# Projections of an attention block: four product banks, one copy for both query tiles, waits for the transposes moved ahead of a product's last matmul

## The reference

```python
x = x + _L0_conv_ref(_gn(x), L0_conv_w, L0_conv_b)        # mixes points inside shifted 8x8 windows
x = x + _L1_conv_ref(_gn(x), ...)

def _L1_conv_ref(x, w_qkv, w_dw, w_pw, w_proj, bn_gamma, bn_beta, bn_mean, bn_var):
    qkv = jnp.einsum('bchw,oc->bohw', x, w_qkv)            # 256 -> 768 channels
    y = lax.conv_general_dilated(qkv, w_dw, ...)           # 5x5, each channel by itself
    y = lax.conv_general_dilated(y, w_pw, ...)             # 1x1 in groups of 8 channels
    mqkv = jnp.concatenate([qkv, y], axis=1)               # 64 heads of 8 channels, N = 4096
    q = relu(mqkv[:, :, :DIM]); k = relu(mqkv[:, :, DIM:2 * DIM]); v = mqkv[:, :, 2 * DIM:]
    v = jnp.pad(v, ((0, 0), (0, 0), (0, 1), (0, 0)), constant_values=1.0)
    vk = jnp.einsum('bhdn,bhen->bhde', v, k)               # sums over all points
    out = jnp.einsum('bhde,bhen->bhdn', vk, q)
    out = out[:, :, :-1] / (out[:, :, -1:] + ATT_EPS)
    ...                                                    # projection, batch norm
```

## Time and profile before

| | us |
|---|---|
| three runs | 2472.43, 2471.01, 2472.25 |
| median | 2472.25 |
| span of the profiled execution | 2473.8 |
| projections in it, first to last product's matmul | 266.9 to 999.3 |
| TensorE busy in the whole span | 2359.6 (95%) |
| VectorE, ScalarE, GpSimd busy in the whole span | 1994.9 (81%), 1495.6 (60%), 1099.8 (44%) |

### The profile page before, as it was taken

One profiled execution on the slowest core, in us unless ns is written; L12 is line 12 of the kernel. 1 busy time (PEld: TensorE's weight loads), 2 busy tenths in 40 slices (PEclk: granted clock), 3 DMA queues, 4 the chain that ended last, 5 costly groups with the idle time before them and its releaser, 6 DMA issues. The chain is left out here.

```text
span 2473.8 us, 66794 instructions
## 1 busy us (share of the span) xinstructions
PE 2359.6 (95%) x25485; PEld 1881.3 (76%) x25485; DVE 1994.9 (81%) x2653; ACT 1495.6 (60%) x1864; POOL 1099.8 (44%) x1476
## 2 busy tenths in 40 slices
PE   5999799999999999799999999999999889999998
PEld 5889688877777887577888888888888656666666
DVE  7887688878788877778888888888888588888775
ACT  5777566666566666566776776677767434433442
POOL 7722387887787878200000000000000068888887
PEclk9999899999999999899999999999999999999999
DMA  7874689988988989988888888888888777777774
GB/s 285 336 301 173 208 295 344 329 293 314 316 288 323 344 299 302 253 196 207 209 209 208 209 210 207 210 208 209 207 208 210 228 243 280 275 275 271 271 272 136
DMA packets 300973, 628.38 MB, mean 254 GB/s; under 512 B 50784, under 2 KB 252256, under 8 KB 291552
## 3 DMA queue, kind: packets, MB, share of 16 engines
q1 hardware_dynamic: 295072, 590.38, 77.5%
q10 hardware_dynamic: 4688, 31.63, 3.6%
q0 software_dynamic: 1008, 3.67, 0.4%
HBM read 327.81 MB, written 300.94 MB: 254 GB/s over the span
## 5 line engine op out<-in xcount | busy, mean ns | idle before, releaser
L1562 PE MATMUL c_ps<-dh,wh 128*128 128x512 f32 x1152 | 465.3, 404 | 15.8 <-DVE wl L1712 9.9
L1477 ACT ACTIVATE dh<-image 128x1632 fp32r<-128x1632 f32 x192 | 301.5, 1570 | 269.9 <-PE c_ps L1562 254.8
L1562 PE MATMUL c_ps<-dh,wl 128*128 128x512 f32 x1152 | 456.4, 396 | 0.0
L1562 PE MATMUL c_ps<-dl,wh 128*128 128x512 f32 x1152 | 454.6, 395 | 1.6 <-issue 1.6
L1921 POOL TENSOR_TENSOR ql<-image,qh 128x1024 fp32r<-128x1024 f32 x1 | 2.4, 2359 | 967.8 <-DVE ql L2152 967.8
L1670 DVE TENSOR_TENSOR dl<-image,dh 128x1632 fp32r<-128x1632 f32 x192 | 356.3, 1856 | 73.9 <-ACT dh L1477 73.9
L1132 PE MATMUL o_ps<-xh,wqh 128*128 128x512 f32 x768 | 319.2, 416 | 11.3 <-issue 8.4
L1909 POOL TENSOR_TENSOR ql<-image,qh 128x1024 fp32r<-128x1024 f32 x126 | 300.9, 2413 | 10.7 <-ACT qh L1940 10.7
L1132 PE MATMUL o_ps<-xl,wqh 128*128 128x512 f32 x768 | 303.5, 395 | 0.0
L1132 PE MATMUL o_ps<-xh,wql 128*128 128x512 f32 x768 | 301.9, 393 | 0.0
L1562 PEld LDWEIGHTS c_ps<-dh,wh 128*128 128x128 f32 x1152 | 218.5, 190 | 68.6 <-DVE wl L1712 10.0
(11 more groups left out here) (212 smaller groups left out, 5107.8 us busy)
## 6 DMA issues: line engine op xcount, KB each, us to landing
qkv_scratch<-stage SPq DMA_DIRECT2D x384, 408.0 KB, 4.7
image<-qkv_scratch SPq DMA_DIRECT2D x189, 816.0 KB, 6.3
yq_scratch<-qy SPq DMA_DIRECT2D x64, 512.0 KB, 6.7
image<-qr_scratch SPq DMA_DIRECT2D x128, 256.0 KB, 6.1
image<-yq_scratch SPq DMA_DIRECT2D x128, 256.0 KB, 5.3
ox<-x_scratch SPq DMA_DIRECT2D x8, 4096.0 KB, 15.3
qr_scratch<-qs SPq DMA_DIRECT2D x126, 256.0 KB, 3.6
out<-ox SPq DMA_DIRECT2D x7, 4096.0 KB, 12.7
```

The lines of the kernel that those rows point to most:

```text
L1477: act.activation(dh[kind][:, :], raw[kind], ACT.Copy).then_inc(hi_ready, 1)
L1562: last = pe.matmul(c_ps[:, m, :], w[hp][:, kind, part, o:o + P], cells[:, :, HALF * dy:HALF * dy + HALF * NB], start=(k == 0), stop=(k == 5))
```

## The change

- `o_ps` has four banks; product j of step n goes to bank (6n + j) % 4. The waits for a free bank change with it: product 0 waits for `kv_ready` of the step before, product 1 for `kv_ready_v`, products 2 and 3 for `q_ready`, product 4 for `kv_ready` and product 5 for `kv_ready_v` of the same step.
- `vk_ps` is now a part of one bank (`psum_ps` in the rows of after), with one start flag for both head groups.
- Both query tiles are copied by one instruction on ScalarE of 1024 elements, after product 5 and after `turned(1)`. VectorE's copy and the semaphore `q_ready_v` are gone.
- `pause` is gone on GpSimd. `edge` is now a tensor_tensor with a broadcast zero as its other operand, and carries the waits itself. `border` follows the first edge of the step.
- The four waits of `turn` stand ahead of the sixth matmul of the product before it (products 2 and 4), so that the eight transposes have no wait of their own.

```diff
-        o_ps = psum("o_ps", [P, 3, 512])
+        NO = 4
+        o_ps = psum("o_ps", [P, NO, 512])
...
-        vk_ps = psum("vk_ps", [P, 2, 512])
+        sum_bank = psum("psum_ps", [P, 512])
+        vk_ps = sum_bank[:, 0:2 * VS].rearrange("p (u n) -> p u n", u=2)
...
+        def bank(n, j):
+
+            return (QT * n + j) % NO
...
                         if n % 2:
-                            pool.tensor_scalar(staged(j0, n, 0, 0, 1), every_second(buf, t0, n, 0, 1), -1.0, None, ALU.mult)
+                            pool.tensor_tensor(staged(j0, n, 0, 0, 1), none, every_second(buf, t0, n, 0, 1), ALU.subtract)
                         else:
-                            pool.tensor_copy(staged(j0, n, 1, HALF - 1, HALF), every_second(buf, t0, n, NB - 1, 1))
+                            pool.tensor_tensor(staged(j0, n, 1, HALF - 1, HALF), every_second(buf, t0, n, NB - 1, 1), none, ALU.add)
...
                         keys_values_free(pool, b, n)
-                        pause(1 + u, n)
+                        if u == 0 and n % 4 < 2:
+                            queries_free(pool, b, n)
                         edge(kv, 2 * u, 2 * u, n)
+                        if u == 0 and n % 4 < 2:
+                            border(n)
...
                         pool.wait_ge(q_ready, g + 1)
-                        pool.wait_ge(q_ready_v, g + 1)
                         queries_free(pool, b, n)
                         at_least(pool, K["qr_stored"][n % 2], 32 * (4 * b + n // 2))
-                        pause(3, n)
...
-                        act.wait_ge(o_full, o0 + 5)
+                        turned(1)
+                        act.wait_ge(o_full, o0 + 6)
                         queries_read(act, g)
-                        act.activation(qw[:, n % 2, 0, :], o_ps[:, 1, :], ACT.Copy).then_inc(q_ready, 1)
-                        turned(1)
+                        act.activation(qw[:, n % 2, :, :], o_ps[:, bank(n, 4):bank(n, 4) + 2, :], ACT.Copy).then_inc(q_ready, 1)
...
-            def product(b, n, j):
+            def product(b, n, j, before_last=None):
...
                     for w, xx in ((wh, xh), (wl, xh), (wh, xl)):
-                        last = pe.matmul(o_ps[:, j % 3, :], w[:, ct, P * t:P * t + P], xx[:, n % 2, ct, :],
+                        if k == 5 and before_last:
+                            before_last()
+                        last = pe.matmul(o_ps[:, bank(n, j), :], w[:, ct, P * t:P * t + P], xx[:, n % 2, ct, :],
...
-            def turn(b, n, u):
-
-
+            def turn_ready(b, n, u):
                 at_least(pe, k_turned, 2 * (NCH * b + n) + u)
                 at_least(pe, v_turned, 2 * (NCH * b + n) + u)
                 pe.wait_ge(kv_ready, 2 * (NCH * b + n) + u + 1)
                 pe.wait_ge(kv_ready_v, 2 * (NCH * b + n) + u + 1)
+
+            def turn(n, u):
...
-                        product(b, n, 2)
-                        turn(b, n, 0)
+                        product(b, n, 2, lambda: turn_ready(b, n, 0))
+                        turn(n, 0)
...
-                        product(b, n, 4)
+                        product(b, n, 4, lambda: turn_ready(b, n, 1))
...
-                        turn(b, n, 1)
+                        turn(n, 1)
...
-                        dve.wait_ge(o_full, QT * g + 6)
-                        queries_read(dve, g)
-                        dve.tensor_copy(qw[:, n % 2, 1, :], o_ps[:, 2, :]).then_inc(q_ready_v, 1)
```

More of the change, by code:

```diff
@@ L767, in projections @@
         vT = sb("vT", [P, 2, 4, NSQ, VS])
-        tick = sb("ptick", [P, 4 * NCH])
+        zero = sb("zero", [P, 1])
         pw_rep = sb("pw_rep", [P, QT, NPH, D])
@@ L790, in projections @@
         kv_ready, q_ready = sem("kv_ready"), sem("q_ready")
-        kv_ready_v, q_ready_v = sem("kv_ready_v"), sem("q_ready_v")
+        kv_ready_v = sem("kv_ready_v")
         kv_diff, kv_odd = sem("kv_diff"), sem("kv_odd")
@@ L891, in _ @@
         def _(pool):
+            pool.memset(zero[:, :], 0.0).then_inc(zeroed, 1)
             pool.memset(vT[:, :, :, :, SQ:VS], 1.0).then_inc(zeroed, 1)
+            pool.wait_ge(zeroed, 2)
+            none = zero[:, :].unsqueeze(1).unsqueeze(2).broadcast_to([P, 4, NB, 1])
             def body(i, last_body):
@@ L896, in body @@
                     b = 2 * i + par
-                    def pause(k, n):
-                        k = NCH * k + n
-                        pool.tensor_tensor(tick[:, k:k + 1], K["ident"][:, 0:1], K["ident"][:, 1:2], ALU.add)
                     def border(n):
                         row = NB * (1 - n // 4)
-                        keys_values_free(pool, b, n)
-                        queries_free(pool, b, n)
-                        pause(0, n)
                         pool.memset(stage[:, n % 2, :, :, :, row, :].rearrange("p t a k x -> p (t a) k x"), 0.0)
@@ L942, in body @@
                     for n in range(NCH):
-                        if n % 4 < 2:
-                            border(n)
                         keys_values(n, 0)
@@ L1045, in key @@
                                 cells_free(act, g)
-                            act.activation(kv[:, n % 2, 2 * u, :], o_ps[:, (2 * u) % 3, :], ACT.Copy).then_inc(kv_ready, 1)
+                            act.activation(kv[:, n % 2, 2 * u, :], o_ps[:, bank(n, 2 * u), :], ACT.Copy).then_inc(kv_ready, 1)
                         def turned(u):
@@ L1073, in body @@
                             pointwise(2)
-                        act.wait_ge(o_full, o0 + 5)
+                        turned(1)
+                        act.wait_ge(o_full, o0 + 6)
                         queries_read(act, g)
-                        act.activation(qw[:, n % 2, 0, :], o_ps[:, 1, :], ACT.Copy).then_inc(q_ready, 1)
-                        turned(1)
+                        act.activation(qw[:, n % 2, :, :], o_ps[:, bank(n, 4):bank(n, 4) + 2, :], ACT.Copy).then_inc(q_ready, 1)
                         if last_body and par == 1 and n == NCH - 1:
                             act.wait_ge(q_ready, g + 1)
-                            act.wait_ge(q_ready_v, g + 1)
                             act.wait_ge(K["qr_stored"][n % 2], 32 * (4 * b + n // 2))
@@ L1107, in _ @@
                 last.then_inc(w_turned, 1)
-            pe.wait_ge(zeroed, 1)
-            def product(b, n, j):
+            pe.wait_ge(zeroed, 2)
+            def product(b, n, j, before_last=None):
                 t = TILES[j]
@@ L1116, in product @@
                 if j == 0:
+                    at_least(pe, kv_ready, 2 * (NCH * b + n))
+                if j == 1:
                     at_least(pe, kv_ready_v, 2 * (NCH * b + n))
+                if j == 2 or j == 3:
                     at_least(pe, q_ready, NCH * b + n)
-                if j == 1:
-                    at_least(pe, q_ready, NCH * b + n)
-                if j == 2:
-                    at_least(pe, q_ready_v, NCH * b + n)
-                if j == 3:
+                if j == 4:
                     pe.wait_ge(kv_ready, 2 * (NCH * b + n) + 1)
-                if j == 4:
+                if j == 5:
                     pe.wait_ge(kv_ready_v, 2 * (NCH * b + n) + 1)
-                if j == 5:
-                    pe.wait_ge(kv_ready, 2 * (NCH * b + n) + 2)
                 k = 0
@@ L1158, in sum_vk @@
                         last = pe.matmul(vk_ps[ch, u, 0:VS], kT[:, u, a, ch], vT[:, u, a, q, :],
-                                         start=(n == 0 and a == 0), stop=(n == NCH - 1 and a == 3))
+                                         start=(n == 0 and u == 0 and a == 0), stop=(n == NCH - 1 and u == 1 and a == 3))
                 if u == 1:
@@ L1276, in value @@
                             cells_free(dve, g)
-                        dve.tensor_copy(kv[:, n % 2, 2 * u + 1, :], o_ps[:, (2 * u + 1) % 3, :]).then_inc(kv_ready_v, 1)
+                        dve.tensor_copy(kv[:, n % 2, 2 * u + 1, :], o_ps[:, bank(n, 2 * u + 1), :]).then_inc(kv_ready_v, 1)
                     def keys_values(n, u):
@@ L1288, in queries @@
                         dve.wait_ge(q_ready, g + 1)
-                        dve.wait_ge(q_ready_v, g + 1)
                         queries_free(dve, b, n)
```

## The result

The changed kernel takes 2485.68 us (median of 4 runs, 2483.11 to 2488.47) against 2471.99 us before (4 runs, 2471.01 to 2472.43): a ratio of 1.0057, 95% interval 1.0044 to 1.007. It is slower by 14 us. The prediction had said 2480 within 2467 to 2492, and slower as the likeliest. So the forecast was +8 us and the runs give +14, at the upper edge of its main case (2475 to 2486).

A forecast was written before the change was run, and what follows sets the result against it. TensorE, busy 98 to 100% in both stretches, was taken to set the stage's end by its own order. The terms 9.2 - 1.0 - 1.5 - 0.5 - 1.4 + 3.2 = +8.0 us gave a median of 2480 us, range 2467 to 2492.

The forecast's parts named there:

- main case: The forecast that the kernel becomes slower, at a median of 2475 to 2486 us; chance 0.50.
- The first transposes: In the loop the moved wait delays the product's last matmul by 0.18 us in 28 steps, 5.5 us; straight code about nothing.
- The second transposes and the port: Moved waits at the second transposes cost 1.5 us in the loop and 2.2 in straight code; GpSimd delaying VectorE adds 3.2.
- the contention: GpSimd's earlier query edge delays VectorE's fourth difference: 0.06 us on average over 55 turns, +3.2 us, between -1 and +12.
- the shared port rules: Rival: GpSimd gets between VectorE's differences in most steps, +0.25 us at some 50 second transposes, 2489, up to 2495; chance 0.17.
- Group norm: VectorE, freed of copies, ends the n = 4 moments 0.6 us earlier; 0.2 us at each of seven group norms goes: -1.0 us.
- The register wait at product 0: A step's first product has three waits for four, saving 0.05 us in each of 32 loop steps: -1.5 us.
- the sums' wait near the end: Near the end the sums no longer wait 1.29 us for a transposes' copy that stood behind a query copy: -0.5 us.
- The fourth bank: The added product bank gives nothing, since no product waits for a bank in the list of waits.
- Earlier stores: GpSimd's copies and the stores come 0.5 to 1.4 us earlier, so four VectorE waits for stores may go: -1.4 us.
- the longest stall: VectorE's first wait for a store before `stage`, 5.4 us, hangs on SyncE's issue of the first eight stores and stays.
- The base: The profiled execution, 2473.8 us, lies 1.55 us above the runs' median of 2472.25, so 2481.8 becomes a median of 2480.2.

The follow-up runs named there:

- e2: The kernel before with only the four waits of each turn moved ahead of the sixth matmul: 2479.44 us, ratio 1.0031.
- e4: The changed kernel with GpSimd's old code, additions included: 2474.95 us, ratio 1.0011 to the kernel before.
- e9: The kernel before with one ScalarE copy of both query tiles, its three product banks and the sums' own bank kept: 2465.16 us, ratio 0.9963.
- e3: The kernel before with GpSimd's part of the change alone (no additions, edges with a zero operand, border after the first edge): 2477.36 us, ratio 1.0017.
- e5: The changed kernel with VectorE's three waits for free cells ahead of its wait for the product: 2481.66 us, ratio 1.0031 to the kernel before.

## Why the prediction was right, and where its terms were off

**The first transposes.** Right in mechanism and size: load 0.12 us after the copy, 0.17 to 0.18 a turn, 28 turns. +5.5 was worked out; the spacings give +4.6 in the changed kernel and +5.1 in e2. Straight code 0, as said.

**The second transposes and the port.** The moved waits were to cost 3.7 us there and the contention, GpSimd lengthening VectorE's work, 3.2, 6.9 together. Measured are 12.8: +8.6 in the loop and +4.3 in straight code. With GpSimd as before (e4) they are 2.7. The wait alone was sized too large (e2: +1.2 for 3.7). The term that failed is the contention. From step 42 I took it that `border` keeps the old distance in half the steps, and came to 0.06 us on average; VectorE's work is longer by 0.16 to 0.20 in most steps. `border` takes 0.34 us of GpSimd and does not fill the gap that two additions of up to 0.65 leave. I had asked how far the edge moves against the last difference alone, not what each of the four differences now meets. GpSimd's part costs the stage 8.3 us in the changed kernel (744.1 against e4's 735.8), and 11 us by the ratios (1.0057 against 1.0011), for 3.2 less 1.4 by my terms. So the rival "the shared port rules" named the true mechanism, and its price of 12 us was near; the total hid it behind gains that I had also sized too small. The Trainium skill (SBUF — State Buffer, "Who interferes with whom") has the rule by which VectorE's two-input instruction and GpSimd's reader exclude each other; the 1.09 us of a difference that takes 0.64 unhit, and the 0.67 to 0.70 of all 128 copies from PSUM, agree with it. GpSimd pays the same way, and its query copy rose from 677 to 1072 ns on average, the first row being before's:

```profile
L935 POOL COPY stage<-qw 128x512 f32<-128x512 f32 x64 | 43.3, 677 | 0.0
```

```profile
L937 POOL COPY stage<-qw 128x512 f32<-128x512 f32 x64 | 68.6, 1072 | 0.0
```

**The gains.** Group norm: -1.0 worked out, -3.3 measured (what the gaps between products 1 and 2 have above the usual 0.23 us: 4.46 before, 1.14 after, over all steps). The step that failed took the stall from the list of waits, 1.6 us for seven of the small matmuls; their weight load had been idle for 0.64 by the row of L161 above, and the spacing of the products around it, 0.86, was there to be read. The register wait at product 0: -1.5 worked out, -3.2 in the loop measured, from a step's last matmul to the second one of the next. I had divided the difference of loop and straight code evenly over four register waits; the gain is nearly twice the 0.05 that came of it. In straight code the same place has -0.3, in which the sums' wait near the end is gone (-0.52, for -0.5 worked out). The fourth bank: nothing, as e9 shows. Earlier stores: VectorE waits 3.6 us less for them in all (8.3 to 4.7 us), of which 2.2 is the longest stall, which I had said would stay; from kernel to kernel that stall moves by more.

**Sum.** At the places of the working, +17.4 for waits and contention and -6.8 for group norm, product 0 and sums make +10.6. My terms for the same places were +12.4 and -3.0, and -1.4 more for stores. Both sides were too small, by 5.0 and 3.8 us, and the errors nearly cancel: that the forecast is better than its terms is luck. What is left of the stage's 11.7 is the 1.2 us by which the loop's back edge is longer from the last product to the next step. The whole step takes 15.5 and 15.6 us in before and e3 and 16.4 to 17.7 in the ten other kernels; none of the rows that I read says why. The last step is 0.8 us longer, and that is the moved wait too: VectorE's late second value now stops product 4, and it is in the +17.4.

**The base.** The text placed the profiled execution 1.55 us above the median of the runs by its span. A run's reported time is 1.7 to 2.0 us above its own span (after: 2483.96 for 2482.2), so that execution lay some 3.5 us above the median. The predicted median hung on the difference alone and is not touched.

**What was to show it.** Load 0.11 after the copy: 0.12. 0.4 or more after the fifth matmul's load: 0.52 (528.63 to 529.15). Value copy in the list ahead of a product's matmul some 50 times: only 10, and the others are among the 100 loads put down to "issue". Matmul 0.32 later: 0.32 and 0.31 for the two spacings. Loop longer by 0.2 to 0.3 us a step: 7.8 / 31 = 0.25. Straight code the same: no, +0.09 to +0.12 a step, less than half. Differences as long as before or longer: longer. Group norm's stall gone: yes.

## What to carry over

Put a wait for the end of another engine's work behind as much of the own queue as the data allow: here a wait one matmul early cost nothing only while its releaser was early, and each further delay of the releaser was then paid in full. Before freeing an engine that shares a port with a busy one, list what each instruction of both will lie beside afterwards, since idle-looking additions can be what keeps two readers apart. And price parts together as well as one by one: here one part was worth -9 us (the query copy on ScalarE, which frees VectorE for the group norm and TensorE of a wait), two cost 5 to 7 us each alone, and together they lie 0.9% above the copy alone.

## What the hardware showed that I had not expected

- With one wait less ahead of product 0, its first matmul starts 0.11 us earlier in the loop (0.92 to 0.81) and 0.03 in straight code (0.72 to 0.69) by the record, but its second only 0.09 and 0.00: read a saving at the second matmul. Three register waits on VectorE cost 0.19 together in the loop, and nothing there where they stand ahead of a longer wait (e5: 0.62 to 0.43).
- A matmul whose load is released late starts 0.03 us after its load by the record, but what comes next follows after 0.31 instead of 0.23: beside its own lateness the load costs 0.08 us.
- Even GpSimd's edge of 64 elements, 0.34 us where no difference is beside it, costs one of VectorE's differences 0.11 to 0.15 (0.64 to 0.75 and 0.78, 0.68 to 0.83); its copy of 512 elements costs 0.45 (0.64 to 1.09, 0.69 to 1.14).
